# The scan's tile loads and stores in scratch memory: tiles laid out in pairs, with one load for two tiles where both hold the same rings

## Chip, core and metric

One of the eight cores of a Trainium2 chip runs the whole program. The metric is the time of one execution on the device in microseconds (us), and lower is better. A core has five engines that run their own instruction streams and meet at semaphores: TensorE (PE; PEld is its weight load), VectorE (DVE), ScalarE (ACT), GpSimd (POOL) and SyncE (SP). Sixteen DMA engines carry all transfers. SP's transfers go through queue q1 and POOL's indirect ones through queue q0.

## What is computed

The input is a batch of 32 images of 56 x 56 positions with 256 channels, all in float32. Two layers follow each other.

```
# layer 0
h = relu(x)
h = depthwise 3x3 convolution of h, dilation 2, + dw_bias
h = h @ pw (256 x 256) + pw_bias
h = h * inv + (beta - mean * inv)          # inv = gamma / sqrt(var + 1e-3)
# layer 1: a scan over the 3136 positions in the order of a spiral from the centre
for each position p:
    local = g[:, p, :]
    neigh = mean of g at the up to 4 neighbours of p    # already updated if they came before p
    u     = concat(local, neigh)                        # 512
    y     = tanh(u @ w1 + b1) @ w2 + b2                 # one number for each image
    g[:, p, :] = local + y * w_y
```

The order of the spiral matters only through `y`: a position needs the `y` of neighbours that came before it, and all else of `u @ w1` can be computed ahead of the scan.

## The kernel before

The program has two phases. In the first, which takes two thirds of the time, the convolution and the products `u @ w1` are computed for 784 blocks of 128 rows (8 columns by 16 images). POOL scatters each block into two scratch tensors in the chip's memory with indirect stores: line 458 puts 256 values a row into `s_x` (the value of layer 0), and line 464 puts 512 values a row into `s_pre` (the hidden layer before the tanh, without the sums over updated neighbours). The table `wave_row` names the row for each partition.

In the second phase, the scan, the 3136 positions are grouped into 897 tiles that follow a wave: position `level` of ring `r` of the spiral is ready when its predecessors on the same ring and on the ring inside are. A tile holds the same level of up to four neighbouring rings, for 32 images each: 128 partitions. `SEQ` is the order of the tiles. A level has `live` tiles, seven at first and one at the end, in stages of 32 levels. `held(c)` gives the quarter range of tile `c` that really holds rings: of the 897 tiles 615 hold all four quarters, and the others one to three.

One tile passes through the engines like this.

- SP loads the tile's 512 values a row from `s_pre` into one of 6 slots of `pre_t` (line 431; slot free when `passed` or `copied` says that the earlier tile was handed over), and four tiles later its 256 values a row from `s_x` into one of 8 slots of `x_t` (line 438; slot free when `out_ready` says that the earlier tile was finished). Both stand in one order on SP's queue. In the trace these loads are called dw_rows<-s_pre and dw_rows<-s_x, since the slots lie in the memory of `dw_rows`.
- PE hands the tile over into a PSUM bank with a product by the identity (`hand_over`, line 901, four tiles ahead), and later adds the neighbour sums to it (`add_sums`, line 912). With two live tiles a level, ACT copies it instead (line 586).
- ACT takes the tanh (line 581).
- DVE forms the dot product with `w2` (`dot`, line 752), the terms of the neighbour sums when a part of a level is complete (`neighbours`, lines 775, 797 and 802), and the tile's result (`finish`, line 760). `finish(c)` waits for the tile's x load and for the store of tile `c - 4` to have landed, because `o_t` has 4 slots.
- PE turns the sums into the next level's weights (`turn`, lines 919 to 921) and ACT copies them (line 590).
- POOL stores the result into `out` with an indirect store (line 476), shown as out<-dw_rows.

The lines that carry the two waits of SP and the wait for the store are these.

```
if c >= PRE_SLOTS:
    back = c - PRE_SLOTS
    sp.wait_ge(copied if by_act(back) else passed, handed(back, by_act(back)))
...
if c >= XT_SLOTS:
    sp.wait_ge(out_ready, c - XT_SLOTS + 1)
...
if c >= OUT_SLOTS:
    dve.wait_ge(tile_out[c % OUT_SLOTS], 16 * (c // OUT_SLOTS))
```

Of the kernel before, what the change touches and what calls it, by code (L numbers as in the profile page):

```python
# [50 lines left out]
WIN = 4  # L51
HIST = PAD + LEVELS + 1
OUT_OF_RANGE = B * H * W
PRE_SLOTS, XT_SLOTS, OUT_SLOTS, BANKS, AHEAD = 6, 8, 4, 6, 4
X_BEHIND = 4
V_ROWS = 4

TERMS = (V_ROWS + 1) * WIN
# [33 lines left out]
def held(c):  # L92

    level, g = SEQ[c]
    qs = [q for q in range(Q) if ring_of(g, q) >= 0 and ring_point(ring_of(g, q), level) is not None]
    assert qs and qs == list(range(qs[0], qs[-1] + 1))
    return qs[0], qs[-1] + 1


def groups_of(part, level):  # L100
# [5 lines left out]
def by_act(c):  # L106

    return live(SEQ[c][0]) == 2
# [33 lines left out]
    return g, q  # L142


def shape_tables():
    where = {ring_point(r, i): (r, i) for r in range(RINGS + 1) for i in range(max(1, 8 * r))
             if ring_point(r, i) is not None}
    assert len(where) == H * W
    img = np.arange(B)
    at_group = {ring_of(g, q): (g, q) for g in range(GROUPS + 1) for q in range(Q)}  # L150

    store_row = np.full((P, TILES), OUT_OF_RANGE, np.int32)
    for c, (level, g) in enumerate(SEQ):
        for q in range(*held(c)):
            y, x = ring_point(ring_of(g, q), level)
            store_row[B * q:B * (q + 1), c] = (img * H + y) * W + x

    wave_row = np.zeros((P, TILES1), np.int32)
    for h in range(HALVES):
        for y in range(H):  # L160
            for w in range(W):
                r, i = where[y, w]
                g, q = at_group[r]
                t, wl = divmod(w, WI)
                b16 = np.arange(NB)
                wave_row[wl * NB + b16, (h * H + y) * T + t] = TILE_AT[i, g] * P + q * B + 2 * b16 + h
    assert len(np.unique(wave_row)) == wave_row.size

    coef = np.zeros((P, N_COEF), np.float32)
    wrap = np.zeros((P, 2, LEVELS // 8), np.float32)  # L170
    for level in range(LEVELS - 1):
        t = level + 1
        for r in range(1, RINGS + 1):
            if ring_point(r, t) is None:
                continue
            g, q = at_group[r]
            part = part_of(t, g)
            g0 = groups_of(part, t)[0]
            y, x = ring_point(r, t)
            near = [where[p] for p in ((y - 1, x), (y + 1, x), (y, x - 1), (y, x + 1)) if p in where]  # L180
            for r2, i2 in [p for p in near if p < (r, t)]:
                g2, q2 = at_group[r2]
                rows = slice(B * q2, B * (q2 + 1))
                if t == 8 * r - 1 and i2 == 0:
                    assert level % 8 == WRAP_LEVEL and wrap_of(level) == (g, q)
                    wrap[rows, 0 if r2 == r else 1, level // 8] = 1.0 / len(near)
                    continue
                d = t - i2
                at = COEF_AT[part, level] + (g2 - g0) * WIN + (7 - d) // 2
                if r2 == r:  # L190
                    assert d == 1
                    coef[rows, at] = 1.0 / len(near)
                else:
                    assert r2 == r - 1 and d in (1, 3, 5, 7) and g2 - g == (q == 0)
                    coef[rows, at + (groups_of(part, t)[1] - g0 + 1) * WIN] = 1.0 / len(near)

    part_i = np.arange(P)

    sel = np.zeros((P, V_ROWS + 5), np.float32)
    j = part_i % IN_AT  # L200
    term = (j < 3 * TERMS) & (part_i < BIAS_AT)
    bias_hi, bias_lo = part_i == BIAS_AT, part_i == BIAS_AT + 1
    for i in range(V_ROWS):
        sel[:, i] = (term & (j % TERMS // WIN == i)) | bias_hi | bias_lo
    sel[:, V_ROWS:] = np.stack([term & (j // TERMS != 1), term & (j // TERMS == 1), bias_hi, bias_lo,
                                bias_hi | bias_lo], 1)
    shift = np.zeros((P, 2, P), np.float32)
    shift[part_i[:P - B], 0, part_i[:P - B] + B] = 1.0
    shift[part_i[P - B:], 1, part_i[P - B:] - (P - B)] = 1.0
    return store_row, wave_row, coef, wrap, sel, shift  # L210
# [35 lines left out]
def build(nc, x, dwk, dwb, pwk, pwb, gamma, beta, mmean, mvar, w1, b1, w2, b2, wy,  # L246
# [7 lines left out]
    with ctx:  # L254
# [3 lines left out]
        def sem(name):  # L258
            return ctx.enter_context(nc.semaphore(name))
# [95 lines left out]
        cleared = sem("cleared")  # L355
        pre_clear = sem("pre_clear")
        v_ready = sem("v_ready")
        pre_in = [sem(f"pre_in{i}") for i in range(PRE_SLOTS)]
        xt_in = [sem(f"xt_in{i}") for i in range(XT_SLOTS)]
        passed = sem("passed")  # L360
        copied = sem("copied")
        pre_ready = sem("pre_ready")
# [32 lines left out]
        def _(sp):  # L395
# [25 lines left out]
            for i in range(EO_SLOTS):  # L421
                sp.wait_ge(e_stored[i], 16 * (TILES1 // EO_SLOTS))
            sp.wait_ge(pre_clear, 1)
            for n in range(TILES + X_BEHIND):
                c = n
                if c < TILES:
                    q0, q1 = held(c)
                    if c >= PRE_SLOTS:
                        back = c - PRE_SLOTS
                        sp.wait_ge(copied if by_act(back) else passed, handed(back, by_act(back)))  # L430
                    sp.dma_start(pre_t[B * q0:B * q1, c % PRE_SLOTS, :],
                                 s_pre[c * P + B * q0:c * P + B * q1, :]).then_inc(pre_in[c % PRE_SLOTS], 16)
                c = n - X_BEHIND
                if c >= 0:
                    q0, q1 = held(c)
                    if c >= XT_SLOTS:
                        sp.wait_ge(out_ready, c - XT_SLOTS + 1)
                    sp.dma_start(x_t[B * q0:B * q1, c % XT_SLOTS, :],
                                 s_x[c * P + B * q0:c * P + B * q1, :]).then_inc(xt_in[c % XT_SLOTS], 16)

        @block.gpsimd
        def _(pool):
# [11 lines left out]
            for tick in range(FIRST_TICK, LAST_TICK + 1):  # L454
                n = tick - ROW_AT - 2
                if 0 <= n < TILES1:
                    pool.wait_ge(xp_copied, n + 1)
                    pool.indirect_dma_start(s_x, bass.IndirectOffsetOnAxis(wave_idx[:, n:n + 1], 0),  # L458
                                            xo[:, n % XO_SLOTS, :], None, bounds_check=TILES * P - 1,
                                            oob_is_err=False).then_inc(x_stored[n % XO_SLOTS], 16)  # L460
                n = tick - ROW_AT - HID_LAG - 2
                if 0 <= n < TILES1:
                    pool.wait_ge(hid_copied, n + 1)
                    pool.indirect_dma_start(s_pre, bass.IndirectOffsetOnAxis(wave_idx[:, n:n + 1], 0),  # L464
                                            eo[:, n % EO_SLOTS, :], None, bounds_check=TILES * P - 1,
                                            oob_is_err=False).then_inc(e_stored[n % EO_SLOTS], 16)

            pool.wait_ge(lo_ready, 4 * ROWS)
# [14 lines left out]
        def _(act):  # L483
# [95 lines left out]
            for c in range(TILES):  # L579
                act.wait_ge(pre_ready, c + 1)  # L580
                act.activation(psum[:, c % BANKS, :], psum[:, c % BANKS, :], ACT.Tanh).then_inc(th_ready, 1)  # L581
                ahead = c + AHEAD
                if ahead < TILES and by_act(ahead):
                    act.wait_ge(pre_in[ahead % PRE_SLOTS], 16 * (ahead // PRE_SLOTS + 1))
                    act.wait_ge(y_ready, ahead - BANKS + 1)
                    act.activation(psum[:, ahead % BANKS, :], pre_t[:, ahead % PRE_SLOTS, :],
                                   ACT.Copy).then_inc(copied, 1)
                for part, level in HIGH_ROWS_AT.get(c, ()):
                    act.wait_ge(s_turned, S_COUNT[part, level])
                    act.activation(s_rows[0:BIAS_AT, part, :], psum[0:BIAS_AT, BANKS + part, 0:P],  # L590
                                   ACT.Copy).then_inc(s_ready, 1)

        @block.vector
        def _(dve):
# [159 lines left out]

            def finish(c):
                dve.wait_ge(y_ready, c + 1)
                dve.wait_ge(xt_in[c % XT_SLOTS], 16 * (c // XT_SLOTS + 1))
                if c >= OUT_SLOTS:
                    dve.wait_ge(tile_out[c % OUT_SLOTS], 16 * (c // OUT_SLOTS))
                dve.scalar_tensor_tensor(out=o_t[:, c % OUT_SLOTS, :], in0=wy_row, scalar=y_of(c),  # L760
                                         in1=x_t[:, c % XT_SLOTS, :], op0=ALU.mult,
                                         op1=ALU.add).then_inc(out_ready, 1)
# [51 lines left out]
        def _(pe):  # L814
# [80 lines left out]
            pe.wait_ge(xp_copied, TILES1)  # L895

            def hand_over(c):
                pe.wait_ge(pre_in[c % PRE_SLOTS], 16 * (c // PRE_SLOTS + 1))
                if c >= BANKS:
                    pe.wait_ge(y_ready, c - BANKS + 1)  # L900
                pe.matmul(psum[:, c % BANKS, :], ident[:, :], pre_t[:, c % PRE_SLOTS, :], start=True,  # L901
# [111 lines left out]
```

## Time and profile before

| what | value |
|---|---|
| median of 3 runs | 4776.31 us (4768.79 to 4791.13) |
| profiled execution, its own time | 4755.92 us |
| its span, first to last instruction | 4754.1 us |
| granted TensorE clock, mean | 0.993 |
| PE busy | 4491.0 us (94%) |
| DVE busy | 3981.0 us (84%) |
| POOL busy | 3445.8 us (72%) |
| ACT busy | 2551.0 us (54%) |
| moved by DMA | 835.52 MB, mean 176 GB/s |
| the first tanh of the scan starts at | 3182.6 us |

The profiled execution is one run with the profiler on; its time and its span differ by 1.8 us, and its time is 20.4 us under the median. Durations below are from it. The mean over the span hides that the two phases differ: the table of stretches below divides the scan into its seven stages.

### The profile page before, as it was taken

The numbers are of one execution on the slowest core, as the hardware profiler recorded it, in microseconds if no ns is written. First come the engines' busy times: TensorE is split into PE (matmuls) and PEld (weight loads), VectorE is DVE, ScalarE is ACT, GpSimd is POOL, SyncE is SP. The second block draws the span as 40 slices with busy tenths as digits, with TensorE's granted clock in tenths as the row PEclk, the third lists the DMA queues.
The fourth block names the chain that finished last, engine by engine and source line by source line (L and its number), as shares of the span: only waits on it lengthen the run. The fifth ranks groups of instructions, "written<-read, shape, count | busy, mean of one in ns | idle before, by whom it ended". The sixth has DMA issues, their size and how long they took to land.

```text
span 4754.1 us, 62034 instructions
## 1 busy us (share of the span) xinstructions
PE 4491.0 (94%) x19609; PEld 3350.7 (70%) x19609; DVE 3981.0 (84%) x5685; ACT 2551.0 (54%) x4523; POOL 3445.8 (72%) x2478
## 2 busy tenths in 40 slices
PE   4999999999999999999999999998888899999889
PEld 3888878888888888888878888864444445555556
DVE  7888888888888788888888888738888888898884
ACT  4566656666666666665656666444344444444552
POOL 1888888888887788888888888756666666665542
PEclk8999999999999999999999999999999999999999
DMA  4344444444444444444444444359999998888751
GB/s 101 124 139 134 133 134 140 132 135 138 131 138 138 129 138 134 131 142 131 132 132 140 132 136 130 151 178 318 303 299 320 296 301 291 287 273 256 209 176 51
DMA packets 394994, 835.52 MB, mean 176 GB/s; under 512 B 76848, under 2 KB 178480, under 8 KB 394544
## 3 DMA queue, kind: packets, MB, share of 16 engines
q1 hardware_dynamic: 249008, 417.52, 31.4%
q0 software_dynamic: 143408, 411.26, 23.2%
q8 instruction: 163, 2.67, 0.2%
q10 hardware_dynamic: 2256, 2.77, 0.2%
q14 instruction: 159, 1.30, 0.1%
HBM read 420.17 MB, written 425.85 MB: 178 GB/s over the span
## 4 chain that ended last, share of the span: by engine, by line
PE 61%; DVE 12%; issue 10%; ACT 7%; DMA 5%; POOL 4%; SPq 0%; DVEq 0%; POOLq 0%; ACTq 0%
PE psum L888 13%; PE psum L890 13%; PE psum L889 13%; PE psum L872 13%; DVE psum L752 5%; DMA out<-dw_rows 4%; DVE dw_rows L760 3%; ACT relu_rows L563 3%; POOL out L476 3%; PE psum L861 3%; PE psum L928 2%; PE psum L912 1%; PE psum L901 1%; DMA s_pre<-eo,wave_idx 1%; PE psum L919 1%
## 5 line engine op out<-in xcount | busy, mean ns | idle before, releaser
L676 DVE SCALAR_TENSOR_TENSOR dw_rows<-relu_rows,taps,dw_rows 128x1792 f32<-128x1792 f32 x872 | 1803.4, 2079 | 6.2 <-issue 5.2
L464 POOL DMA_INDIRECT s_pre<-eo,wave_idx x784 | 1327.0, 1693 | 249.7 <-issue 224.2
L458 POOL DMA_INDIRECT s_x<-xo,wave_idx x784 | 1215.2, 1550 | 377.5 <-issue 233.8
L476 POOL DMA_INDIRECT out<-dw_rows x897 | 899.8, 1003 | 677.2 <-issue 401.3
L888 PE MATMUL psum<-w_hi,u_hi 128*128 128x512 f32 x3136 | 1383.4, 441 | 0.0
L890 PE MATMUL psum<-w_hi,u_lo 128*128 128x512 f32 x3136 | 1231.8, 393 | 0.0
L889 PE MATMUL psum<-w_lo,u_hi 128*128 128x512 f32 x3136 | 1224.7, 391 | 0.0
L517 ACT ACTIVATE eo<-psum 128x512 f32<-128x512 f32 x784 | 468.1, 597 | 1218.6 <-PE psum L890 1160.9
L901 PE MATMUL psum<-dw_rows,ident 128*128 128x512 f32 x1666 | 885.0, 613 | 98.1 <-DVE near L752 74.7
L872 PE MATMUL psum<-pw,dw_rows 128*128 128x256 f32 x3136 | 818.8, 384 | 61.6 <-ACT psum L572 44.9
L581 ACT ACTIVATE psum<-psum 128x512 f32<-128x512 f32 x897 | 522.0, 582 | 545.8 <-PE psum L912 283.7
L752 DVE CUSTOM_DVE_ANT_0 psum<-psum,dw_rows,b_col 128x512 f32<-128x512 f32 x897 | 676.4, 754 | 112.8 <-ACT psum L581 106.4
L872 PEld LDWEIGHTS psum<-pw,dw_rows 128*128 128x128 f32 x3136 | 570.7, 190 | 183.1 <-issue 103.3
L890 PEld LDWEIGHTS psum<-w_hi,u_lo 128*128 128x128 f32 x3136 | 589.7, 188 | 137.9
L889 PEld LDWEIGHTS psum<-w_lo,u_hi 128*128 128x128 f32 x3136 | 592.2, 189 | 122.5
L888 PEld LDWEIGHTS psum<-w_hi,u_hi 128*128 128x128 f32 x3136 | 591.8, 189 | 117.9
L912 PE MATMUL psum<-u_hi 128*128 128x512 f32 x897 | 620.1, 691 | 43.1 <-ACT u_hi L590 33.7
L726 DVE TENSOR_TENSOR u_lo<-near,u_hi 128x1024 fp32r<-128x1024 f32 x224 | 243.7, 1088 | 384.6 <-ACT u_hi L541 257.3
L760 DVE SCALAR_TENSOR_TENSOR dw_rows<-dw_rows,near 128x256 f32<-128x256 f32 x897 | 434.0, 484 | 126.7 <-DMA out<-dw_rows 80.5
L901 PEld LDWEIGHTS psum<-dw_rows,ident 128*128 128x128 f32 x1666 | 269.0, 189 | 336.0 <-issue 317.0
L563 ACT ACTIVATE relu_rows<-psum 128x896 f32<-128x896 f32 x224 | 414.6, 1855 | 20.7 <-DMA dwb_c<-L_conv_dw_bias 10.6
L572 ACT ACTIVATE psum<-bias_all 128x256 f32<-128x256 f32 x782 | 332.5, 425 | 5.6
(90 smaller groups left out, 3913.6 us busy)
## 6 DMA issues: line engine op xcount, KB each, us to landing
dw_rows<-s_pre SPq DMA_DIRECT2D x615, 256.0 KB
x_tok<-x SPq DMA_DIRECT2D x112, 896.0 KB
dw_rows<-s_x SPq DMA_DIRECT2D x615, 128.0 KB
dw_rows<-s_pre SPq DMA_DIRECT2D x169, 192.0 KB
dw_rows<-s_x SPq DMA_DIRECT2D x169, 96.0 KB
out<-dw_rows POOLq DMA_INDIRECT x897
s_x<-xo,wave_idx POOLq DMA_INDIRECT x784
s_pre<-eo,wave_idx POOLq DMA_INDIRECT x784
```

What stands on the lines that cost most here:

```text
L458: pool.indirect_dma_start(s_x, bass.IndirectOffsetOnAxis(wave_idx[:, n:n + 1], 0), xo[:, n % XO_SLOTS, :], None, bounds_check=TILES * P - ...
L464: pool.indirect_dma_start(s_pre, bass.IndirectOffsetOnAxis(wave_idx[:, n:n + 1], 0), eo[:, n % EO_SLOTS, :], None, bounds_check=TILES * P - 1,
L476: pool.indirect_dma_start(out_rows, bass.IndirectOffsetOnAxis(store_idx[:, c:c + 1], 0), o_t[:, c % OUT_SLOTS, :], None, bounds_check=OUT_ ...
L676: dve.scalar_tensor_tensor(out=dst, in0=pair_rows(relu_rows, k + ky - 1, c, 2 * kx * NB), scalar=taps[:, c, 3 * ky + kx:3 * ky + kx + 1], ...
L752: dve.tensor_tensor_reduce(out=bank, in0=bank, in1=w2_row, scale=1.0, scalar=b2_col[:, 0:1], op0=ALU.mult, op1=ALU.add, accum_out=y_of(c)) ...
L760: dve.scalar_tensor_tensor(out=o_t[:, c % OUT_SLOTS, :], in0=wy_row, scalar=y_of(c), in1=x_t[:, c % XT_SLOTS, :], op0=ALU.mult, op1=ALU.ad ...
L872: last = pe.matmul(bank, dw_rows[:, R % D_SLOTS, c, NB + P * t:NB + P * (t + 1)], pw[:, c, :], start=False, stop=c == CK - 1, skip_group_c ...
L888: pe.matmul(bank, hi, w_hi[:, k, :], start=k == 0, stop=False)
L889: pe.matmul(bank, hi, w_lo[:, k, :], start=False, stop=False)
L890: last = pe.matmul(bank, lo, w_hi[:, k, :], start=False, stop=k == 2 * CK - 1)
L901: pe.matmul(psum[:, c % BANKS, :], ident[:, :], pre_t[:, c % PRE_SLOTS, :], start=True, stop=False).then_inc(passed, 1)
L912: pe.matmul(psum[:, c % BANKS, :], s_rows[:, part, :], v_sel[:, row, :], start=False, stop=True, skip_group_check=by_act(c)).then_inc(pre_ ...
```

## The change

Two tiles `2j` and `2j + 1` now share 256 rows of each scratch tensor, and row `p` of one lies beside row `p` of the other. The stores of the first phase keep their number and their sizes; only the row numbers in `wave_row` change. On the way back, a pair is loaded by one transfer if both tiles hold the same quarters: each partition then gets 4096 B in one piece from `s_pre` (2048 B before) and 2048 B from `s_x` (1024 B before). If they hold different quarters, each tile has its own transfer, with rows of the old size and twice the old distance.

Worked out from `held`, 244 of the 448 full pairs are loaded whole: 88, 72, 36, 32, 4, 1 and 13 of them in the stages with seven, six, five, four, three, two and one live tiles. SP's loads in the scan go from 1794 to 1306.

The rings of slots are in pairs too. `pre_t` has 10 slots instead of 6 and `x_t` 12 instead of 8, and a semaphore belongs to a pair of slots. SP waits until both earlier tiles of a pair of slots are done, and the x load stands two pairs behind the other, as it stood four tiles behind. The memset of `pre_t` ahead of the scan (line 733) covers 10 slots.

```
-PRE_SLOTS, XT_SLOTS, OUT_SLOTS, BANKS, AHEAD = 6, 8, 4, 6, 4
-X_BEHIND = 4
+PRE_SLOTS, XT_SLOTS, OUT_SLOTS, BANKS, AHEAD = 10, 12, 4, 6, 4
+PRE_PAIRS, XT_PAIRS = PRE_SLOTS // 2, XT_SLOTS // 2
+X_BEHIND = 2
...
+PAIRS2 = (TILES + 1) // 2
+def pair_loads(j):
+    tiles = [c for c in (2 * j, 2 * j + 1) if c < TILES]
+    if len(tiles) == 2 and held(tiles[0]) == held(tiles[1]):
+        return [(tiles[0], 2) + held(tiles[0])]
+    return [(c, 1) + held(c) for c in tiles]
+def loaded(c, pairs):
+    j = c // 2
+    return 16 * sum(len(pair_loads(i)) for i in range(j % pairs, j + 1, pairs))
...
+def pair_row(c, p):
+    return (c // 2 * P + p) * 2 + c % 2
...
-                wave_row[wl * NB + b16, (h * H + y) * T + t] = TILE_AT[i, g] * P + q * B + 2 * b16 + h
+                wave_row[wl * NB + b16, (h * H + y) * T + t] = pair_row(TILE_AT[i, g], q * B + 2 * b16 + h)
...
+            for n in range(PAIRS2 + X_BEHIND):
+                j = n
+                if j < PAIRS2:
+                    if j >= PRE_PAIRS:
+                        back = 2 * (j - PRE_PAIRS)
+                        for c in (back, back + 1):
+                            sp.wait_ge(copied if by_act(c) else passed, handed(c, by_act(c)))
+                    for c, tiles, q0, q1 in pair_loads(j):
+                        at = c % PRE_SLOTS
+                        sp.dma_start(pre_t[B * q0:B * q1, at:at + tiles, :],
+                                     pre_pairs[j * P + B * q0:j * P + B * q1, c % 2:c % 2 + tiles, :]).then_inc(
+                                         pre_in[j % PRE_PAIRS], 16)
+                j = n - X_BEHIND
+                if j >= 0:
+                    if j >= XT_PAIRS:
+                        sp.wait_ge(out_ready, 2 * (j - XT_PAIRS) + 2)
+                    for c, tiles, q0, q1 in pair_loads(j):
...
-                    act.wait_ge(pre_in[ahead % PRE_SLOTS], 16 * (ahead // PRE_SLOTS + 1))
+                    act.wait_ge(pre_in[ahead // 2 % PRE_PAIRS], loaded(ahead, PRE_PAIRS))
...
-                dve.wait_ge(xt_in[c % XT_SLOTS], 16 * (c // XT_SLOTS + 1))
+                dve.wait_ge(xt_in[c // 2 % XT_PAIRS], loaded(c, XT_PAIRS))
...
-                pe.wait_ge(pre_in[c % PRE_SLOTS], 16 * (c // PRE_SLOTS + 1))
+                pe.wait_ge(pre_in[c // 2 % PRE_PAIRS], loaded(c, PRE_PAIRS))
```

## Rows read from the trace of the kernel before

**Rows 1.** The page: 40 slices of the span, busy share of each in tenths.

```profile
PE   4999999999999999999999999998888899999889
DVE  7888888888888788888888888738888888898884
DMA  4344444444444444444444444359999998888751
```

**Rows 2.** Busy time in the stages with seven, six, five, four live tiles.

```profile
core 0: us, PE busy (x) PEld busy (x) DVE busy (x) ACT busy (x) POOL busy (x), PEclk, DMA share, GB/s
3184.00:3543.00 359.00, 315.70 (x1050) 158.61 (x1048) 297.93 (x867) 144.85 (x287) 220.99 (x221) 1.00 0.94 309
3545.00:3850.00 305.00, 272.37 (x955) 140.65 (x954) 258.80 (x769) 125.54 (x254) 190.67 (x191) 1.00 0.93 305
3852.00:4104.00 252.00, 232.59 (x862) 131.40 (x860) 220.22 (x675) 108.63 (x222) 160.57 (x159) 0.99 0.89 290
4106.00:4305.00 199.00, 190.99 (x759) 112.93 (x758) 183.27 (x580) 91.32 (x191) 133.38 (x128) 1.00 0.90 284
```

**Rows 3.** The same stretches, the tanh (line 581) alone: one for each tile.

```profile
3184.00:3543.00 359.00, 130.10 (x224) 1.00 0.94 309
3545.00:3850.00 305.00, 110.78 (x191) 1.00 0.93 305
3852.00:4104.00 252.00, 92.54 (x159) 0.99 0.89 290
4106.00:4305.00 199.00, 73.96 (x128) 1.00 0.90 284
```

**Rows 4.** Waits in 3184 to 3543 us: total, times, longest.

```profile
PE psum L901 <- DVE near L752: 38.7, 60, 2.1
DVE dw_rows L760 <- DMA out<-dw_rows: 33.7, 52, 2.2
DVE dw_rows L760 <- issue: 15.7, 25, 1.7
PE psum L901 <- issue: 3.4, 11, 0.5
SPq L438 <- DVE dw_rows L760: 51.7, 58, 2.1
```

**Rows 5.** One store in the timeline and in the chain.

```profile
3502.90 0.48 DVE L760 SCALAR_TENSOR_TENSOR dw_rows<-dw_rows,near 128x256 f32<-128x256 f32 x1
3504.54 5.07 DMA out<-dw_rows
3509.73 0.48 DVE dw_rows L760
3323.89 6.95 DMA out<-dw_rows
4750.02 0.97 POOL L476 DMA_INDIRECT out<-dw_rows  x1 [0.30 <-issue]
```

**Rows 6.** DMA queues in 3184 to 3543 us.

```profile
q1 hardware_dynamic: 61358, 83.31, 74.0%
q0 software_dynamic: 10549, 27.17, 19.4%
```

**Rows 7.** DMA in 3176 to 3178 us: loads of `s_pre` alone.

```profile
DMA packets 406, 0.74 MB, mean 370 GB/s; under 512 B 45, under 2 KB 45, under 8 KB 406
```

**Rows 8.** First phase: DMA in 1095 to 1098.5 us, and the stores issued.

```profile
q1 hardware_dynamic: 107, 0.77, 91.2%
1093.34 1.69 POOL L464 DMA_INDIRECT s_pre<-eo,wave_idx  x1 [0.30 <-issue]
```

**Rows 9.** DMA from 1098.5 to 1101 us.

```profile
q0 software_dynamic: 211, 0.68, 75.0%
```

**Rows 10.** Timeline between the phases.

```profile
3150.67 3.19 DVE L733 MEMSET dw_rows<- 128x512 f32 x6 [2.00 <-PE psum L872]
3173.85 2.23 SPq L431 DMA_DIRECT2D dw_rows<-s_pre  x5
```

More of the change, by code:

```diff
@@ L357, in build @@
         v_ready = sem("v_ready")
-        pre_in = [sem(f"pre_in{i}") for i in range(PRE_SLOTS)]
-        xt_in = [sem(f"xt_in{i}") for i in range(XT_SLOTS)]
+        pre_in = [sem(f"pre_in{i}") for i in range(PRE_PAIRS)]
+        xt_in = [sem(f"xt_in{i}") for i in range(XT_PAIRS)]
         passed = sem("passed")
@@ L423, in _ @@
             sp.wait_ge(pre_clear, 1)
[L424 to L439, printed above, removed]
+            pre_pairs = s_pre.rearrange("(r o) n -> r o n", o=2)
+            x_pairs = s_x.rearrange("(r o) n -> r o n", o=2)
+            for n in range(PAIRS2 + X_BEHIND):
[15 more added lines that the diff above has]
+                    for c, tiles, q0, q1 in pair_loads(j):
+                        at = c % XT_SLOTS
+                        sp.dma_start(x_t[B * q0:B * q1, at:at + tiles, :],
+                                     x_pairs[j * P + B * q0:j * P + B * q1, c % 2:c % 2 + tiles, :]).then_inc(
+                                         xt_in[j % XT_PAIRS], 16)
         @block.gpsimd
@@ L458, in _ @@
                     pool.indirect_dma_start(s_x, bass.IndirectOffsetOnAxis(wave_idx[:, n:n + 1], 0),
-                                            xo[:, n % XO_SLOTS, :], None, bounds_check=TILES * P - 1,
+                                            xo[:, n % XO_SLOTS, :], None, bounds_check=2 * PAIRS2 * P - 1,
                                             oob_is_err=False).then_inc(x_stored[n % XO_SLOTS], 16)
@@ L464, in _ @@
                     pool.indirect_dma_start(s_pre, bass.IndirectOffsetOnAxis(wave_idx[:, n:n + 1], 0),
-                                            eo[:, n % EO_SLOTS, :], None, bounds_check=TILES * P - 1,
+                                            eo[:, n % EO_SLOTS, :], None, bounds_check=2 * PAIRS2 * P - 1,
                                             oob_is_err=False).then_inc(e_stored[n % EO_SLOTS], 16)
@@ L1006 @@
         aps.append(nc.dram_tensor(n, a.shape, mybir.dt.from_np(a.dtype), kind="ExternalInput").ap())
-    s_pre = nc.dram_tensor("s_pre", (TILES * P, HID), mybir.dt.float32, kind="Internal").ap()
-    s_x = nc.dram_tensor("s_x", (TILES * P, C), mybir.dt.float32, kind="Internal").ap()
+    s_pre = nc.dram_tensor("s_pre", (2 * PAIRS2 * P, HID), mybir.dt.float32, kind="Internal").ap()
+    s_x = nc.dram_tensor("s_x", (2 * PAIRS2 * P, C), mybir.dt.float32, kind="Internal").ap()
     out = nc.dram_tensor("out", (B, H, W, C), mybir.dt.float32, kind="ExternalOutput").ap()
```

## The prediction

> **What bounds the kernel now.** I read the page's 40 slices first. The DMA row stands at 3 or 4 tenths in the first phase and at 9 from the scan's start on, and falls again at its end [rows 1]. Nothing in the first phase is a load from scratch, and its stores keep number and size, so the change can only act in the scan, from 3182.6 us on, and there mainly where DMA is full.
>
> Second come the windows by stage, divided by the tanh count, which is one for each tile [rows 2, 3]. Seven live tiles: 359 us / 224 = 1.603 us a tile, with DMA busy for 0.94 of it (1.51 us), PE 315.7 / 224 = 1.41 us, DVE 297.9 / 224 = 1.33 us. Six: 1.597 us a tile, DMA 0.93, PE 1.43, DVE 1.35. Five: 1.585, DMA 0.89, PE 1.46, DVE 1.39. Four: 1.555, DMA 0.90, PE 1.49 (96% of the time), DVE 1.43. So with seven and six live tiles no compute engine is full and DMA nearly is; with four, PE is the bound. The later stages have fewer bytes a tile still and long waits from tile to tile; I put their change at nothing.
>
> Third, who waits. The loads are early: PE waits only 3.4 us for something that the profile can't name (a late `s_pre` load would be there) in 359 us. DVE's `finish` waits 33.7 us for stores into `out` (52 times) and 15.7 us more for something unnamed (25 times) [rows 4]. The stores have 4 slots, so `finish` of a tile and `finish` four tiles on make a loop. One turn of it in the trace: `finish` starts at 3502.90, POOL issues the store at 3504.54, it lands after 5.07 us, and the next `finish` of that slot starts at 3509.73: 6.83 us, where four tiles take 6.41 us on average. Other stores take up to 6.95 us. The last store of the kernel, alone on the DMA engines, goes from 4750.02 to before the end at 4754.1, under 4.1 us [rows 5]. So a full DMA shows itself as slow stores, and slow stores hold DVE, and through the PSUM banks PE (38.7 us on line 752) [rows 4].
>
> **The sum, part by part.**
>
> *Transfer rate.* In the first stage q1, the loads, has 74.0% of the engines' time: 83.31 MB in 0.740 x 359 x 16 = 4251 us, so 19.6 B/ns on each engine. The stores, which go in packets of four 1024 B rows (27.17 MB in 10549 packets, completion writes among them), have 27.17 MB in 1114 us: 24.4 B/ns [rows 6]. Loads of 2048 B rows alone ran at 370 GB/s, 23.1 B/ns an engine [rows 7]. A full tile brings 256 KB + 128 KB, 24576 B to an engine: 24576 / 19.6 = 1.25 us. Loaded in pairs, I put the 4096 B rows at the stores' rate and the 2048 B rows at that of the pure loads: 16384 / 24.4 + 8192 / 23.1 = 0.67 + 0.355 = 1.03 us. That would save 0.23 us a tile, if all the loss of rate lies in the row size; if it lies in two kinds of traffic mixing, it saves nothing. I take the middle, 0.11 us, and keep 0 and 0.23 for the range.
>
> The Trainium skill ("DMA: Bandwidth & Descriptors", section "Why small descriptors are slow (HBM only)") gives about 3 cycles of overhead to each packet beside one cycle for 32 bytes. By that, an estimate from the page, rows of 1024 B going to 2048 B save 4% and rows of 2048 B going to 4096 B 2%, together about 0.03 us a tile, and the change would gain some 12 us before any price. The rates in the trace differ by far more, but they don't say why.
>
> *What a gain in DMA time is worth.* At a DMA share of 0.94, 0.11 us less is 0.117 us less a tile for tiles in whole pairs. Those are 176 of 225 tiles, 144 of 192 and 72 of 160 in the first three stages: 0.091, 0.088 and 0.053 us on the average tile. PE is the next bound. If it could be 96% busy, as it is with four live tiles, the periods would end at 1.41 / 0.96 = 1.468, 1.485 and 1.524 us, so at most 0.135, 0.112 and 0.061 us can be gained. The gains lie under these caps: 0.091 x 225 + 0.088 x 192 + 0.053 x 160 = 20.5 + 16.9 + 8.5 = 46 us. The caps give 30 + 21.5 + 10 = 62 us.
>
> *Longer loads ahead of a store.* At 1095.03 us POOL had finished issuing a store of the first phase. From 1095 to 1098.5 us q1 has 91.2% of the engines' time with 107 of its packets, an `x_tok` load of 896 KB that gives each engine 8 rows, and no packet of q0 moves; from 1098.5 to 1101 us q0 has 75.0% [rows 8, 9]. So a store waits until a load's rows on its engine are through. A whole pair puts 8 rows of 4096 B on an engine (1.3 us) where 8 rows of 2048 B (16384 / 23.1 = 0.71 us) stood, and 0.71 us where about 0.35 us stood. A store behind the one waits up to 0.7 us longer, behind the other up to 0.35 us, and met at a random place half of that, 0.26 us on average. Four tiles share it: 0.065 us a tile when the loop through the store sets the pace. DVE waited there for 77 of 224 tiles; a faster pace makes the loop bind more often, so I count two thirds, 0.043 us on 392 tiles = 17 us. The ends are 0 (loads and stores fall into different halves of the 3.2 us of a pair) and the slower rival below.
>
> The Trainium skill (same page, "Queues, rings and completion order") says that each engine takes turns between the queues a packet at a time, with whole packets drained. By a strict reading a store of few packets would pass an 8-row load after one or two of its rows, and the price would be a few tenths of this. The rows of the first phase show longer waits, and I go by them.
>
> *Other parts.* The waits by pairs come later, but the rings are deeper: an `s_pre` load may be issued when the tile 9 before it was handed over (6 now), an `s_x` load when the tile 11 before was finished (8 now), so loads stay early. SP has 488 fewer loads to issue, hidden, since SP waits 51.7 us for DVE in the first stage [rows 4]. SP's two kinds of load now are released by different tiles of a pair, so bursts of both together should be rare; I give nothing for it. Four more memsets of 0.53 us each put the end of line 733 at 3156.0, long before the first load at 3173.85: hidden [rows 10]; without the cover 2.1 us. The first x load stands behind six tiles of `s_pre` instead of five, 0.7 us, hidden by the first `hand_over` products; at most 1 us. Single loads with rows at twice the distance: nothing, as their rows keep their size; the five-live stage, with most of its pairs split, carries the doubt. Indirect stores of the first phase to rows twice as far apart: nothing, since PE, not DMA at 4 tenths, is busy there [rows 1].
>
> *Sum.* -46 + 17 = -29 us. The profiled execution took 4755.92 us by its own time (span 4754.1), so 4727 in its terms; it lies 20.4 us under the median of the runs, and against that median, 4776.31, I forecast 4748 us.
>
> **Rivals.** A measurement here tells a change from none at about 0.5%, 24 us.
>
> A. *DMA time falls and the scan speeds up*, 4748 us, own range 4708 to 4760. For it: DMA at 0.94 while PE and DVE have 0.2 us a tile to spare. Chance 0.42.
>
> B. *It cancels, or there was little to save*: the rate hardly depends on the rows' size (the page's overhead gives 12 us against the 17 us of longer loads), or the store loop takes back what the rate gives. PE never waits for a load, which speaks for it, too. 4752 to 4800 us, about 4776. Chance 0.34.
>
> C. *Stores stuck behind whole pairs set the pace*, the case on the other side. Stores of every other tile fall behind an `s_pre` pair and wait the whole 0.71 us more; their loop takes 6.41 + 0.71 = 7.12 us, 1.78 us a tile, 0.18 us more on 392 tiles: +70 us, 4846 us. If every store waited 0.71 + 0.35 us more, 1.87 us a tile and +104 us, 4880 us. It decides from an added wait of 4 x 0.091 = 0.36 us a store, where the gain in rate is used up. For it: the loop has no slack with seven live tiles, and the first phase shows that a store doesn't get in between. Against it: less load time leaves q1 idle more often. Chance 0.24.
>
> **Range and chances.** 4708 (the caps, and a little noise) to 4850 (C at its first price). Part of A's own range lies within 24 us of the median, and a little of B below it: faster by over 0.5% 0.40, within 0.5% 0.36, slower 0.24.
>
> **What the profile after would show.** For the rate: in the first stage q1 has clearly fewer packets (about 35,000 to 40,000 for the same bytes) and over 21 B/ns. For its worth: the tanh count in 359 us over 235, PE over 92%, DVE's wait for out<-dw_rows not longer. For C: that wait doubled, stores of over 6 us in the chain, DMA share under 0.85 and the period above 1.65 us. The prediction is wrong in its root if the stages with four and fewer live tiles or the first phase move by more than 10 us.

## The result, and the profile after

The changed kernel is slower: 4827.83 us median (4815.88 to 4832.09, 5 runs) against 4777.89 us of the kernel before (4768.79 to 4791.13, 5 runs). The ratio is 1.0098, with a 95% interval of 1.0075 to 1.012. The time lies in the predicted range only because the range reached up to rival C's price: the forecast was a faster kernel, 29 us down, and what came is 0.98% up, 47 us, two thirds of C's 70 us. The chance given to slower by over 0.5% was 0.24.

The profiled execution took 4821.91 us (span 4820.1), 66 us over that of before. The page of the kernel after, its head and the DMA queues:

```profile
PE 4507.2 (94%) x19609; PEld 3365.2 (70%) x19609; DVE 3981.2 (83%) x5689; ACT 2551.5 (53%) x4523; POOL 3477.8 (72%) x2478
...
DMA  4344444444444444444444443469899888887651
...
q1 hardware_dynamic: 179888, 417.49, 30.7%
```

The DMA row has 9 no longer through the scan [rows 1]: the engines for transfers are less full, and the time is longer.

The first and last tanh of the kernel after (line 612 here), then the windows of its first two stages, with all instructions (PE, PEld, DVE, ACT, POOL busy, clock, DMA share, GB/s) and with the tanh alone:

```profile
L612 ACT ACTIVATE psum<-psum x897: 565/582/592, 3204.9 to 4812.1; 128x512 f32<-128x512 f32 x180
...
3206.00:3575.00 369.00, 320.23 (x1051) 163.96 (x1050) 296.79 (x868) 145.22 (x287) 225.40 (x221) 0.97 0.91 303
3577.00:3894.00 317.00, 274.82 (x955) 146.00 (x953) 257.24 (x770) 125.54 (x254) 193.94 (x192) 0.98 0.89 293
...
3206.00:3575.00 369.00, 130.33 (x224) 0.97 0.91 303
3577.00:3894.00 317.00, 110.58 (x190) 0.98 0.89 293
```

With seven live tiles a level the tile takes 369 / 224 = 1.647 us (1.603 before), with six 1.668 us (1.597) [rows 2, 3]. DMA's share fell from 0.94 and 0.93 to 0.91 and 0.89. The first tanh starts 22.3 us later than before; whether that is the change is asked below. From the first tanh to the last it is 1607.2 us here.

The waits of the first stage in the kernel after, the DMA queues there, and the five longest pieces of its chain:

```profile
DVE dw_rows L791 <- DMA out<-dw_rows: 42.0, 49, 2.8
DVE dw_rows L791 <- issue: 12.6, 17, 1.9
PE psum L932 <- DVE near L783: 44.0, 55, 2.6
...
q1 hardware_dynamic: 36399, 84.23, 72.0%
q0 software_dynamic: 10559, 27.19, 18.9%
...
3235.17 6.04 DMA out<-dw_rows
3362.38 6.40 DMA out<-dw_rows
3408.84 5.76 DMA out<-dw_rows
3444.16 6.39 DMA out<-dw_rows
3480.41 6.04 DMA out<-dw_rows
```

The packets of q1 fell from 61358 to 36399 for the same bytes, as forecast, but its rate is 84.23 MB / (0.720 x 369 x 16 us) = 19.8 B/ns on an engine, where it was 19.6 [rows 6]. DVE's wait in `finish` for stores is 42.0 us for 33.7; with the part that the profile can't name, 12.6 for 15.7, it is 54.6 for 49.4 [rows 4]. That the unnamed part is a wait for stores too is not shown, but in e7, which differs from the kernel before only in the depth of the rings for loads, all 49.7 us are named as stores. So the sums are compared below.

Of the signs that the prediction named, the four-live stage took 210 us for its 128 tiles (202 before, from the first tanh of the stage to the first of the next) and the three later ones together took as long as before within 1 us. Both are under the 10 us named there.

### The profile page after: what moved, and what is told of

It reads as the page before. It is cut to its first block, busy times and chain, and to the rows that moved or that the text cites. A ratio compares the mean times of both kernels' runs of the same rounds, so it can differ in the third digit from the quotient of the medians.

```text
span 4820.1 us, 61994 instructions
## 1 busy us (share of the span) xinstructions
PE 4507.2 (94%) x19609; PEld 3365.2 (70%) x19609; DVE 3981.2 (83%) x5689; ACT 2551.5 (53%) x4523; POOL 3477.8 (72%) x2478
## 3 DMA queue, kind: packets, MB, share of 16 engines
q0 software_dynamic: 143408, 411.26, 22.9%
## 4 chain that ended last, share of the span: by engine, by line
PE 59%; DVE 12%; issue 11%; DMA 7%; ACT 7%; POOL 4%; SPq 0%; DVEq 0%; POOLq 0%; another core or an unknown queue 0%; ACTq 0%
PE psum L919 12%; PE psum L921 12%; PE psum L920 12%; PE psum L903 12%; DMA out<-dw_rows 6%; DVE psum L783 5%; DVE dw_rows L791 3%; ACT relu_rows L594 3%; PE psum L892 3%; PE psum L932 2%; POOL out L507 2%; PE psum L959 2%; PE psum L943 1%; POOL s_pre L495 1%; DMA s_pre<-eo,wave_idx 1%
## 5 line engine op out<-in xcount | busy, mean ns | idle before, releaser
L489 POOL DMA_INDIRECT s_x<-xo,wave_idx x784 | 1287.1, 1642 | 376.0 <-issue 219.7
L495 POOL DMA_INDIRECT s_pre<-eo,wave_idx x784 | 1280.5, 1633 | 246.9 <-issue 227.8
L594 ACT ACTIVATE relu_rows<-psum 128x896 f32<-128x896 f32 x224 | 413.7, 1850 | 20.5 <-DMA dwb_c<-L_conv_dw_bias 10.7
```

## The experiments

All ratios are to the kernel before, on the same chip, with 95% intervals; e8 had 3 rounds, the others 5. Three chips were used: one for e1 to e4 and e13 to e16, one for e5 to e8, one for e9 to e12.

| label | what | ratio |
|---|---|---|
| e1 | after, no pair loaded whole | 1.0044 (1.0031 to 1.0057) |
| e2 | before, pair rows in scratch | 1.0055 (1.0043 to 1.0067) |
| e3 | before, 8 slots for the result | 0.9715 (0.9702 to 0.9727) |
| e4 | after, 8 slots for the result | 0.9717 (0.9705 to 0.973) |
| e5 | after, only pairs of `s_x` whole | 1.0033 (1.0021 to 1.0045) |
| e6 | after, only pairs of `s_pre` whole | 1.0112 (1.0093 to 1.0131) |
| e7 | before, rings of 10 and 12 | 0.9993 (0.9984 to 1.0002) |
| e8 | before, 3 slots for the result | 1.0423 (1.0407 to 1.0439) |
| e9 | after on the old rows, whole pairs | 1.0094 (1.0079 to 1.0108) |
| e10 | after on the old rows, none whole | 1.0016 (1.0006 to 1.0025) |
| e11 | before, `s_pre` alone in pair rows | 1.0049 (1.0036 to 1.0061) |
| e12 | before, `s_x` alone in pair rows | 1.0015 (1.0004 to 1.0026) |
| e13 | before, `s_pre` loads in two halves | 1.025 (1.0233 to 1.0266) |
| e14 | after, `s_pre` loads in two halves | 1.0203 (1.0184 to 1.0222) |
| e15 | before, 5 slots for the result | 0.9788 (0.9772 to 0.9805) |
| e16 | after, 5 slots for the result | 0.9875 (0.9856 to 0.9894) |

### The change taken apart: e1 and e2

```
# e1, on the kernel after
-    if len(tiles) == 2 and held(tiles[0]) == held(tiles[1]):
+    if False:
# e2, on the kernel before
+                wave_row[...] = pair_row(TILE_AT[i, g], q * B + 2 * b16 + h)
-                                 s_pre[c * P + B * q0:c * P + B * q1, :])
+                                 pre_pairs[c // 2 * P + B * q0:c // 2 * P + B * q1, c % 2, :])
# and s_x likewise
```

> The changed kernel, but every tile is loaded by a transfer of its own; the pair rows, the pair-wise waits and the rings of 10 and 12 slots stay. Theory 1 (stores wait behind the 512 KB loads): the scan gets its time back, total 0 to 0.3% over the kernel before, first stage near 1.60 us a tile. Theory 2 (release by pairs makes the loads lumpy, whoever moves them): stays about 1% over the kernel before, first stage at 1.65 us a tile. Theory 3 (rows at twice the distance slow the transfers): also stays about 1% over, with q1's rate down.

> The kernel before with only the row numbers changed: the first phase scatters to pair rows, the scan loads single tiles with rows at twice the distance, rings and waits as before. Theory 3 (row distance): about 1% slower, part of it as a first phase longer by 10 to 20 us (first tanh near 3200 us). Theories 1 and 2: within 0.2% of the kernel before, first tanh within the scatter of unchanged kernels.

None of the three theories had it alone. The pair rows by themselves cost 0.55%; on top of them, with the pair-wise waits, it is 0.44%, and loading whole pairs adds the other 0.54% to 1.0098. The profile of e2 shows where the rows cost. Its tanh, its window and its wait in the first stage:

```profile
L588 ACT ACTIVATE psum<-psum x897: 567/582/582, 3176.3 to 4774.5; 128x512 f32<-128x512 f32 x180
...
3178.00:3547.00 369.00, 316.44 (x1050) 159.06 (x1049) 296.89 (x866) 144.72 (x287) 222.67 (x222) 0.99 0.92 301
...
DVE dw_rows L767 <- DMA out<-dw_rows: 62.4, 81, 2.0
```

The first phase is no longer (the first tanh at 3176.3, 3182.6 before); the scan is, 1598.2 us between the first and last tanh for 1563.6 (3182.6 to 4746.2) before. So the first phase's 22 us in the profile after isn't shown to be the change: among kernels with pair rows the first tanh stood at 3176.3 (e2), 3175.9 (e4), 3202.7 (e1) and 3204.9 us (after), and with the old rows at 3182.6 (before), 3193.6 (e3) and 3194.4 (e7). Against the 49.4 us of before (33.7 named, 15.7 unnamed), the wait for stores in e2's first stage is 13 us longer, and the stage is 10 us longer.

### Is the store loop the bound: e3, e4, e8, e15, e16

```
# e3 on the kernel before, e4 on the kernel after; e8: 3, e15 and e16: 5
-... OUT_SLOTS, BANKS, AHEAD = ..., 4, 6, 4
+... OUT_SLOTS, BANKS, AHEAD = ..., 8, 6, 4
# e3, e4, e15, e16: the slots lie in x_tok, which the scan doesn't use
-        o_t = in_dw.take(OUT_SLOTS * C)...
+        o_t = x_tok[:, :, :].rearrange("p a b -> p (a b)")[:, 0:OUT_SLOTS * C]...
```

> The kernel before with 8 slots for the result in place of 4 (they lie in the memory of x_tok, free in the scan). If the loop finish, store, landing, finish holds DVE in the first three stages, as the prediction said, DVE's wait for out<-dw_rows nearly vanishes and 40 to 60 us go (1%). If DMA's total load is the bound and the wait only its symptom, the wait moves to the loads and the gain is under 15 us.

> The changed kernel with 8 slots for the result. Theory 1 (stores stuck behind pairs): with the store's time no longer in the loop, the change costs nothing against the kernel before with 8 slots, or gains 0 to 30 us by its fewer transfers. Theory 2 (lumpy release): it stays 30 to 50 us over the kernel before with 8 slots.

> The kernel before with 3 slots for the result in place of 4. If the loop over the store sets the pace, the first stage takes the loop over 3 tiles: with 6.4 us a turn 2.1 us a tile, with 5.6 us (less traffic in between) 1.87 us, so 0.27 to 0.5 us more on about 700 tiles, 190 to 350 us, ratio 1.04 to 1.07. If DMA's total were the bound, nearly nothing would change.

> The kernel before with 5 slots for the result (in the memory of x_tok). 3 slots gave 1.0423 and 8 gave 0.9715. The loop of 6.4 us over 5 tiles is 1.28 us, under the 1.32 us at which PE is full, so most of the 2.85% should be there already: 0.972 to 0.980.

> The changed kernel with 5 slots for the result. The loop stands closer to PE's own pace than with 8 slots, so if its stores take longer, a part of the price is left: 0.2 to 0.5% over the kernel before with 5 slots; with 8 it was none.

This is the largest effect of the study, and over twice the 40 to 60 us expected of e3. With 8 slots the kernel before takes 4618.42 us for 4749.89 (chip of that run), and the changed kernel 4614.94 us: the whole price of the change is gone, and it brings no gain either. The first stage of e3, window, DMA view's mean with queues, and what is left of the wait:

```profile
3195.00:3490.00 295.00, 293.59 (x1050) 161.31 (x1049) 286.38 (x868) 144.80 (x287) 222.45 (x220) 1.00 1.04 374
...
DMA packets 71804, 110.45 MB, mean 373 GB/s; under 512 B 11007, under 2 KB 38114, under 8 KB 71778
...
q1 hardware_dynamic: 61379, 83.31, 80.3%
...
DVE x_tok L760 <- issue: 0.6, 2, 0.3
PEld psum L901 <- DMA dw_rows<-s_pre: 13.8, 34, 0.9
```

The same 224 tiles, with loads of the old size and row, pass in 295 us, 1.317 us a tile. DMA moves 373 GB/s where it moved 309 [rows 2], and q1 has the same 83.31 MB in 0.803 x 296 x 16 = 3803 us, 21.9 B/ns for 19.6. PE is busy for 99.5% and DVE for 97%: these are probably the next bound. A share of 0.94 was not a full DMA, and 1.41 us a tile was not PE's need. The share here is over 1, so it is no plain share of time either.

The number of slots sets the pace as a loop does. The windows of the first stages of e8 (3 slots) and e15 (5 slots), and the waits of e15 and e16:

```profile
3181.00:3602.00 421.00, 327.51 (x1050) 161.80 (x1049) 301.79 (x867) 145.08 (x287) 222.35 (x221) 0.98 0.84 264
```

```profile
3184.00:3496.00 312.00, 302.67 (x1050) 157.93 (x1048) 291.11 (x866) 144.56 (x287) 226.16 (x221) 1.00 1.01 355
DVE x_tok L760 <- DMA out<-x_tok,dw_rows: 12.2, 32, 0.8
```

```profile
DVE x_tok L791 <- DMA out<-x_tok,dw_rows: 36.2, 53, 2.0
```

With 224 tiles in each, 3, 4, 5 slots give 1.879, 1.603 and 1.393 us a tile. One turn of the loop (slots times time a tile) is then 5.6, 6.4 and 7.0 us: it grows slower than the slots. DMA moves 264, 309 and 355 GB/s meanwhile, so more traffic meets a store at the faster pace; that this lengthens the turn is not shown apart. With 5 slots the changed kernel is 0.9% slower than the kernel before (0.9875 for 0.9788), as with 4, and not the 0.2 to 0.5% expected; its DVE waits 36.2 us for stores there, for 12.2. Three more slots, and both are equal. One slot more had already given 2.1% of the 2.85%. With 5 and 8 slots they also lie in other memory (`x_tok`), and 4 slots there were not run; e8, with 3 slots in the old place, follows the same loop, so the number of slots is enough to explain it.

### Which load, and is it its length: e5, e6, e9, e10

```
# e5: s_pre singly, s_x in pairs; e6: the other way round
+def pair_loads(j, merge=True): ... if merge and len(tiles) == 2 and ...
# e9, on the kernel after: old row numbers, pairs read from two places
-                wave_row[...] = pair_row(TILE_AT[i, g], q * B + 2 * b16 + h)
+                wave_row[...] = TILE_AT[i, g] * P + q * B + 2 * b16 + h
-            pre_pairs = s_pre.rearrange("(r o) n -> r o n", o=2)
+            pre_pairs = s_pre.rearrange("(j o p) n -> j p o n", o=2, p=P)
# e10: e9 and if False: in pair_loads
```

> The changed kernel, but only the pairs of s_x are loaded whole (2048 B rows, 8 of them on a DMA engine take 0.7 us); tiles of s_pre are loaded singly. Never merged stood at 1.0044 of the kernel before, all merged at 1.0098. Theory 1 (a store waits until the load ahead of it is through, so the price goes with the length of the load): about a third of the 0.54%, ratio near 1.006. A rival by count (what costs is that two tiles come at once, whatever their size): half of it, 1.007. No effect of x: 1.0044.

> The changed kernel, but only the pairs of s_pre are loaded whole (4096 B rows, 8 of them take 1.3 us). Theory 1: about two thirds of the 0.54% of merging, ratio near 1.008, and the landings of the stores of even and odd tiles differ. By count: 1.007.

> The changed kernel on the rows of the kernel before: a tile's rows lie together in scratch, and a whole pair is still one transfer of 512 KB and one of 256 KB, but in rows of 2048 B and 1024 B, 16 of them on each DMA engine, read from two places. Theory 1 (the length of a load ahead of a store costs): against the next kernel 0.5 to 0.7% more, as merging cost on pair rows. Theory 4 (what costs is the single row of 4096 B, since merging s_x to 2048 B was free): no more than the next kernel.

> The same rows as before, every tile loaded singly, but released and waited for by pairs, with rings of 10 and 12 slots. On pair rows this stood at 1.0044, with pair rows and single release at 1.0055. Theory 2 (release by pairs costs): over 1.003. If the row distance made all of the 0.5%: 0.997 to 1.001.

Merging `s_x` costs nothing (1.0033 for 1.0044), merging `s_pre` costs 0.68% (1.0112 for 1.0044). The price isn't in proportion to length. The rival by count, two tiles at once whatever their size, would have had `s_x` pairs cost half, and they cost nothing.

e9 against e10 is the cleanest pair: the same releases, rings and bytes, and the same rows of 2048 and 1024 B in both; only that 512 KB of `s_pre` come as one transfer or as two of 256 KB one behind the other, and 256 KB of `s_x` as one or as two of 128 KB, which by e5 is free on pair rows. One transfer costs 0.78% more. e10 itself stands at 1.0016: release by pairs with the deeper rings costs 0.16%, under the 0.3% that theory 2 asked for and over the 1.001 of the other. The row of 4096 B is cleared (theory 4 fell). First stage of e9, then of e10:

```profile
3193.00:3560.00 367.00, 314.10 (x1050) 161.64 (x1048) 294.63 (x868) 145.06 (x287) 226.03 (x221) 0.98 0.92 304
DVE dw_rows L791 <- DMA out<-dw_rows: 62.2, 72, 2.6
...
3335.52 6.51 DMA out<-dw_rows
```

```profile
3187.00:3544.00 357.00, 314.19 (x1051) 160.59 (x1050) 294.95 (x868) 145.05 (x287) 224.86 (x222) 0.99 0.95 313
DVE dw_rows L791 <- DMA out<-dw_rows: 51.0, 64, 2.6
...
3308.78 6.28 DMA out<-dw_rows
```

For the same 224 tiles 10 us more, and 11.2 us more of DVE's wait for stores: the time of one transfer of 512 KB goes through that wait. It does so over the whole scan, too. The table has, from each profile, DVE's idle time ahead of all 897 `finish` instructions and the time from the first tanh to the last, in us.

| kernel | idle ahead of `finish` | scan |
|---|---|---|
| before | 124 | 1564 |
| e7, deeper rings | 116 | 1556 |
| e12, `s_x` in pair rows | 124 | 1568 |
| e11, `s_pre` in pair rows | 134 | 1575 |
| e2, both in pair rows | 153 | 1598 |
| e10, old rows, none whole | 131 | 1571 |
| e9, old rows, pairs whole | 160 | 1597 |
| e6, only `s_pre` whole | 171 | 1613 |
| after | 155 | 1607 |
| e8, 3 slots | 304 | 1763 |
| e3, 8 slots | 1 | 1422 |

Both columns move together: down to e6 the two differences from the kernel before agree within 5 us. In the kernel after, 13 of the 44 us stand elsewhere. The idle time also tells which stores are late. Of the first 225 tiles, the even ones have 25.7 us and the odd ones 26.0 before, 41.8 and 9.2 in e10, and 52.4 and 10.9 in e9. So release by pairs alone moves the wait to every other tile at nearly the same sum, and whole pairs add to it there. The expectation of e6, a difference between even and odd tiles, came true (52.0 and 13.8), but e1 has one already (42.1 and 11.5).

### Rings and row distance: e7, e11, e12

```
# e7
-PRE_SLOTS, XT_SLOTS, ... = 6, 8, ...
+PRE_SLOTS, XT_SLOTS, ... = 10, 12, ...
# e11: e2 for s_pre alone; e12: e2 for s_x alone; the other tensor has a table
# wave_old of old row numbers, loaded beside wave_row
```

> The kernel before with rings of 10 and 12 slots for the loads in place of 6 and 8, all else as before. If the loads were ever late it gains. By the store loop the loads' depth does nothing, or costs a little since more loads may be queued ahead of a store: 0.998 to 1.004, while a gain over 0.5% would say that loads matter.

> The kernel before with only s_pre in pair rows (single loads of 2048 B rows, 4096 B apart); s_x keeps its rows and an index table of its own. If the distance costs by bytes or by row, s_pre has two thirds or half of the 0.55%: 1.003 to 1.004. If only one of the two tensors matters, 1.000 or 1.0055.

> The kernel before with only s_x in pair rows (single loads of 1024 B rows, 2048 B apart). By the same count: 1.002 to 1.003, or 1.000 or 1.0055 if only one tensor matters. The DVE wait for stores in the first three stages should move by as much as the time.

Deeper rings are worth nothing (0.9993, an interval that holds 1): late loads did not hold the kernel before. The row distance costs 0.49% with `s_pre` and 0.15% with `s_x`, together the 0.55% of e2 within their intervals; the larger part is `s_pre`. The wait for stores of e11 and e12 in the first stage (370 and 357 us for 224 tiles), where e12 has no more of it than before (49.4 us):

```profile
DVE dw_rows L770 <- DMA out<-dw_rows: 60.6, 84, 2.8
```

```profile
DVE dw_rows L770 <- DMA out<-dw_rows: 49.4, 81, 2.8
```

### Shorter transfers: e13 and e14

```
# both; e13 on the kernel before, e14 on the kernel after
+                    mid = B * (q0 + q1) // 2
+                    for r0, r1 in ((B * q0, mid), (mid, B * q1)):
+                        sp.dma_start(pre_t[r0:r1, ...], s_pre[... r0 ... r1, :])
```

> The kernel before with each s_pre load cut into two of 64 partitions (4 rows of 2048 B on each DMA engine). Bytes, packets, rings and releases are as before, only the transfers are shorter. Theory 1 in the form that the runs left (a store gets in at the end of a transfer, so the longest transfer sets its wait): DVE's wait for stores falls and the ratio is 0.994 to 0.998. If only transfers over 256 KB hurt: 1.000. If the number of transfers costs: over 1.002.

> The changed kernel with each s_pre load cut into two of 64 partitions: a pair is two transfers of 256 KB, with rows of 4096 B, 4 of them on each engine. Theory 1: the price of merging s_pre goes, the ratio falls from 1.0098 to near that of merging s_x alone, 1.0033 to 1.005. If the rows of 4096 B or the joint release were the cause, it stays at 1.009 to 1.011.

Both were slower by far, and neither tells what it was meant to. In e13 another bound took over. Its waits in the first stage and SP's issues for one tile:

```profile
PEld psum L903 <- DMA dw_rows<-s_pre: 168.0, 173, 2.1
DVE dw_rows L762 <- DMA out<-dw_rows: 2.5, 7, 0.9
...
3302.28 1.10 SPq L433 DMA_DIRECT2D dw_rows<-s_pre  x2
3303.43 0.58 SPq L440 DMA_DIRECT2D dw_rows<-s_x  x1
3304.06 1.14 SPq L433 DMA_DIRECT2D dw_rows<-s_pre  x2
```

Three issues a tile keep SP's queue for 1.10 + 0.58 us and the gaps between them, 1.78 us from one tile to the next; the stage takes 400 us for its tiles. The loads are late now, and DVE hardly waits for stores. In e14 SP had time (it waited 124.6 us for PE in the stage), and the transfers themselves were slower. Its first stage, and its queues:

```profile
3190.00:3585.00 395.00, 323.04 (x1049) 164.66 (x1047) 296.87 (x864) 144.75 (x287) 222.91 (x221) 0.97 0.99 284
...
q1 hardware_dynamic: 38773, 84.60, 77.2%
q0 software_dynamic: 10554, 27.17, 21.8%
```

DMA is busy for 0.99 and moves less, 284 GB/s for 303. The stores have 27.17 MB in 0.218 x 395 x 16 = 1378 us, 19.7 B/ns, for 24.4 before [rows 6], though their packets are the same. In e13, with the same half-width transfers of 2048 B rows, the stores had 27.19 MB in 0.179 x 400 x 16 = 1146 us, 23.7 B/ns. So loads over 64 partitions with rows of 4096 B slow all traffic here, and with rows of 2048 B hardly the stores; why is open. The Trainium skill ("DMA: Bandwidth & Descriptors", section "Rules for kernel authors") advises against two transfers to disjoint halves of the partitions and for one of 128; both runs agree, at 2.5% (e13) and, from 0.98% with whole-width transfers, 2.03% (e14).

## Why the prediction was wrong

*What bounds the kernel.* Half right. The loop finish, store, landing, finish with its 4 slots was read rightly, and e3, e8 and e15 show it. The step that failed is the sentence that a full DMA shows itself as slow stores, which made DMA the bound and the loop its symptom. It is the other way round: the loop holds the pace, and DMA was 0.94 busy beside it. The profile before had a sign: the longest pieces of the chain were stores of 5 to 7 us [rows 5], and PE lost next to nothing to loads.

*Transfer rate*, the term of -46 us, rests on that sentence, and no part of it came. Whole pairs did not bring q1 above 20 B/ns; what brought it to 21.9, with the old rows, was a faster scan (e3). The same packets took 4251 us before and 3803 us in e3, so their recorded time contains waiting, and bytes by busy time isn't the queue's capacity. (The 23.1 B/ns of the pure loads, besides, divides by the whole time of the 2 us window. By busy time, as the other two rates, it is 0.74 MB in 1.070 x 2 x 16 = 34.2 us, 21.6 B/ns.) Where the loop is out of the way, whole pairs do raise the rate: q1 has 83.67 MB in 0.781 x 293 x 16 = 3661 us in e4, 22.9 B/ns for e3's 21.9, which is 0.05 us a full tile. It buys no time even there. The term for the kernel's time was 0, not -46, as the lower bound of the text had it.

*The caps from PE's busy time* were wrong too. PE's 1.41 us a tile fell to 1.31 in e3 without any change to its work. Busy time of PE, which waited often here, was no measure of its need.

*Longer loads ahead of a store*, the term of +17 us: the right mechanism in that the price goes through DVE's wait for stores, and the wrong size and form. Merging cost 0.54% on pair rows and 0.78% on the old ones, 26 to 37 us, within the intervals all of it in the 512 KB loads and none in the 256 KB ones. The share that the text gave to `s_x` pairs is 0. The Trainium skill's rule of turns a packet at a time ("DMA: Bandwidth & Descriptors", "Queues, rings and completion order"), read with one row as a packet, as the profile counts q1's and as the prediction read it, would make one transfer and two of the same bytes, released together, nearly alike: e9 and e10 are not. The same section of the Trainium skill puts about 9 to 17 descriptors into a typical packet. If a load's rows on an engine went as one packet, e9's 16 rows would be one turn where e10's are two, which has the right sign. No trace here shows where the turns fall.

*Single loads with rows at twice the distance*, taken as nothing: 0.55%, 26 us, when all loads are single (e2), and the only large term that the text had no rival for. It too stands in the wait for stores (62.4 us in e2, 49.4 before). How much of it is left in the changed kernel depends on the order in which the parts are put together. There only 409 of the 897 tiles are loaded singly, and the changed kernel, 1.0098, is no slower within the intervals than e9, 1.0094, which merges the same pairs on the old rows.

*Other parts.* Rings, waits by pairs and the memset at nothing: right within 0.2% (e7, e10); the longer memset is 5.35 us and ends at 3177.2 in the profile after, long before the first load at 3195.1. The first phase at nothing: nothing shows otherwise (e2, e4); its 22 us in the profile after are over the 10 us of the prediction's sign, but within the scatter of single profiles. The count of whole pairs by stage sums to 246, two over the true 244, since two pairs that lie across a border between stages are counted in both; this moves nothing.

*The sum.* The 47 us measured (0.98% of 4777.89) can be put together on the old rows: 8 us for release by pairs and the rings (e10, 0.16%), 37 us for one transfer for a pair (e9 over e10, 0.78%) and 2 us for the pair rows (0.04%, not clear of 0). Through the pair rows it is 26 us for the rows (e2), -5 us for release by pairs and the rings (e1, not clear of 0) and 26 us for merging. On either way the rate gives 0 where the text had -46, and merging 26 to 37 where it had +17. Rival C gave 70 us and the right place, DVE's wait at every other tile; its point of decision, a gain in rate used up, had no gain to use up. Of its four signs one came, stores of over 6 us in the chain, and the kernel before had one of those (6.95 us [rows 5]). The wait was not doubled (54.6 us for 49.4), the DMA share was 0.91 and not under 0.85, and the period, 1.647 us, just missed 1.65. So C had the path and not the size.

*What stays open.* Why a transfer of 512 KB holds up a store longer than two of 256 KB behind one another, and why loads with rows 4096 B apart make stores into another tensor land later. e13 and e14 were meant for the first; e13 ran into SP's issues, and e14 into slower transfers. A part of the time in the stages may also be a lower granted clock: 0.97 and 0.98 in the first two stages after, 1.00 before [rows 2]. In the trace it is short stretches at 0.50, the lower level of 1.2 GHz: five in the first stage after, 20.5 us in all, and one of 3.4 us before. Four of the five begin in or within 1.1 us after a wait of PE for a free bank of 1.8 to 2.6 us. Before, a wait of 2.1 us near 3378 us had no such fall behind it. PE's busy time for the same products rose from 315.7 to 320.2 us in that stage. No run separates the clock from the waits.

## What to carry to other kernels

A high DMA share beside a ring of few slots doesn't say that DMA is the bound. Read one turn of the ring from the trace (here 6.83 us) against the period times the slots (6.41 us) first, and if they agree, add a slot before anything else: one more slot of 1 KB a partition gave 2.1%, and four more gave 2.85% (4618.42 us; the changed kernel with 8 slots, 4614.94 us, is the same within the intervals). While the ring was the bound here, merging loads had nothing to give: it saved issues on a queue that had time, was free with `s_x`, and with `s_pre` it made stores late.

## What the hardware showed beside

- One transfer of 512 KB and two of 256 KB, issued one after the other with the same rows, differ by 0.78% of the kernel's time (e9, e10). The first stage is 10 us longer by it, and the wait for another queue's stores there 11.2 us.
- Single loads with rows at twice the distance cost 0.55% (e2); row sizes and bytes were the same.
- Release by pairs, with single loads, moved DVE's wait for stores to the even tiles: 41.8 us against 9.2 in e10, 25.7 against 26.0 before.
- The turn of the store's ring grows with the pace: 5.6 us at 264 GB/s, 6.4 at 309, 7.0 at 355.
- SP took 1.78 us a tile to issue three loads (e13). Loads on 64 partitions with 4096 B rows slowed the stores of the other queue from 24.4 to 19.7 B/ns (e14); with 2048 B rows the stores stood at 23.7 (e13).
- The first tanh came at 3175.9 to 3204.9 us in the profiles, at 3175.9 in one and 3204.9 in another of two kernels whose first phases are alike (e4, after): single profiles can differ by 29 us in a phase that no edit touches.
